# A Macaron block on one NeuronCore: two adapter matrices summed by TensorE, bias additions moved, and the last value product split in float32r parts

## The reference, cut to what matters

```python
x = x + 0.5 * ffn(layernorm(x))      # sum over 8 chosen adapters of weights[k] * W[ids[k]], and their biases
x = x + attn(layernorm(x))           # RWKV time mixing with a recurrence over tokens, then channel mixing
x = x + 0.5 * ffn(layernorm(x))      # the same adapters again
# channel mixing: kk = square(relu(xk @ Wck.T)), hidden size 1024
#                 out = sigmoid(xr @ Wcr.T) * (kk @ Wcv.T)
```

## Time and profile before

| | us |
|---|---|
| median of 3 runs | 431.5 (431.36 to 431.73) |
| the profiled execution, its own time | 431.73 |
| its span, first to last instruction | 429.9 |
| PE busy | 417.1 (97%), 2042 instructions |
| DVE / ACT / POOL busy | 367.9 / 329.7 / 185.6 |

### The profile page before, as it was taken

One profiled execution on the slowest core, in us unless ns is written; L12 is line 12 of the kernel. 1 busy time (PEld: TensorE's weight loads), 2 busy tenths in 40 slices (PEclk: granted clock), 3 DMA queues, 4 the chain that ended last, 5 costly groups with the idle time before them and its releaser, 6 DMA issues.

```text
span 429.9 us, 6308 instructions
## 1 busy us (share of the span) xinstructions
PE 417.1 (97%) x2042; PEld 337.0 (78%) x2042; DVE 367.9 (86%) x725; ACT 329.7 (77%) x669; POOL 185.6 (43%) x194
## 2 busy tenths in 40 slices
PE   8989989889999999999999999999999999999996
PEld 8865875568868887798769886888779876988985
DVE  2988989998989999998989998999999898886235
ACT  1157977899799969997899979997999489945420
POOL 1446052727272635635372728263553347033011
PEclk9999999999999999999999999999999999999999
DMA  6992010001000110002000200010000000000101
GB/s 200 376 398 81 2 49 0 0 2 52 0 0 2 57 44 0 0 26 74 2 0 25 74 1 2 0 50 1 2 0 25 26 0 2 25 26 0 50 2 50
DMA packets 15972, 18.52 MB, mean 43 GB/s; under 512 B 1083, under 2 KB 13635, under 8 KB 15939
## 3 DMA queue, kind: packets, MB, share of 16 engines
q1 hardware_dynamic: 14538, 17.05, 11.4%
q10 hardware_dynamic: 1400, 1.07, 0.8%
HBM read 13.92 MB, written 4.19 MB: 42 GB/s over the span
## 4 chain that ended last, share of the span: by engine, by line
PE 77%; DVE 1%; issue 0%; ACT 0%; DVEq 0%
PE pair L484 22%; PE pair L362 10%; PE pair L374 10%; PE pair L458 6%; PE pair L459 6%; PE pair L462 6%; PE pair L352 6%; PE pair L343 4%; PE pair L499 3%; PE pair L428 1%; PE pair L432 1%; PE pair L429 1%; PE pair L514 0%; DVE rwkv L1054 0%; DVE work L1048 0%
## 5 line engine op out<-in xcount | busy, mean ns | idle before, releaser
L484 PE MATMUL pair<-wcv_sb,kk 128*128 128x256 f32 x448 | 100.4, 380 | 0.0
L484 PEld LDWEIGHTS pair<-wcv_sb,kk 128*128 128x128 f32 x448 | 83.8, 190 | 11.3 <-ACT kk L741 0.7
L458 PE MATMUL pair<-xck_hi,wck_hi 128*128 128x512 f32 x128 | 54.4, 425 | 0.0
L462 PE MATMUL pair<-xck_lo,wck_hi 128*128 128x512 f32 x128 | 50.7, 396 | 0.0
L459 PE MATMUL pair<-xck_hi,wck_lo 128*128 128x512 f32 x128 | 50.6, 395 | 0.0
L737 ACT ACTIVATE kk<-pair 128x512 f32<-128x512 f32 x64 | 36.3, 589 | 14.2 <-PE pair L462 13.3
L1349 POOL TENSOR_TENSOR x2b<-xs,bias_bc 128x512 f32<-128x512 f32 (+1 forms) x16 | 21.8, 1364 | 56.6 <-DVE xcr_lo L1127 22.9
L1349 POOL TENSOR_TENSOR x<-x,bias_bc 128x512 f32<-128x512 f32 x14 | 18.1, 1296 | 55.7 <-DVE rwkv L1054 36.3
L741 ACT ACTIVATE kk<-kk 128x512 f32<-128x512 f32 x64 | 35.9, 625 | 0.0
L1389 POOL TENSOR_TENSOR xs<-x,xa 128x512 f32<-128x512 f32 x16 | 20.4, 1273 | 31.6 <-DVE xa L1060 31.0
L1309 POOL TENSOR_TENSOR rstd_x<-vare_x,nhalf 128x4 f32<-128x4 f32 (+2 forms) x26 | 27.3, 1050 | 9.1 <-DVE vare_x L909 7.8
(11 more groups left out here) (173 smaller groups left out, 1119.3 us busy)
## 6 DMA issues: line engine op xcount, KB each, us to landing
x<-in_x_dram SPq DMA_DIRECT2D x8, 512.0 KB, 4.0
out_dram<-xs SPq DMA_DIRECT2D x15, 256.0 KB, 2.1
xt<-in_xt_dram SPq DMA_DIRECT2D x4, 512.0 KB, 8.2
work<-in_ffn_w_dram ACTq DMA_DIRECT2D x4, 256.0 KB, 5.1
work<-in_ffn_w_dram SPq DMA_DIRECT2D x4, 256.0 KB, 5.2
kk<-in_wck_dram SPq DMA_DIRECT2D x1, 1024.0 KB, 9.6
xs<-in_xt_dram SPq DMA_DIRECT2D x2, 512.0 KB, 10.8
wcv_sb<-in_wcv_dram SPq DMA_DIRECT2D x1, 1024.0 KB, 12.5
```

Source lines behind the costliest of these rows:

```text
L458: nc.tensor.matmul(key_bank(n), wck_hi[:, h, cols], xck_hi[:, h, :], start=h == 0, stop=False)
L462: last = nc.tensor.matmul(key_bank(n), wck_hi[:, h, cols], xck_lo[:, h, :], start=False, stop=h == CH - 1)
L484: last = nc.tensor.matmul(bank_of("kv", e, i)[:, t % TB * C:(t % TB + 1) * C], kk[:, n, tok:tok + P], wcv_sb[:, n, :], start=n == 0, stop= ...
```

## The change

It has four parts.

1. **Adapters.** POOL's queue loads adapters 6 and 7, SP and ACT three each (their biases stay where they were). DVE makes four gated copies of the centring matrices (scaled by the gates of adapters 0 and 1) in `normed`, and PE multiplies adapters 0 and 1 by them straight into PSUM; DVE sums only adapters 2 to 7. PE's warm-up is 16 matmuls ahead of this and 8 behind it instead of 40. The bias product and ACT's copy of it come behind the centred matrix instead of ahead.
2. **Statistics.** `ON_ACT` becomes 1: the statistics of batch 1 move from DVE to ACT, behind `setup_second`. The three memsets of the recurrence's pads move behind `bias_to_first`.
3. **Bias sums on POOL in the loop.** Both halves of `bias_to_x(f + 1)` now wait for `den_done` only; the half 0 of `bias_to_x2` moves to the end of the loop's pass, behind `xcr_done`.
4. **Last values.** For batch 7 the product is split: ACT squares each `kk` tile twice (once into `kk_hi`, once in place), DVE subtracts to get `kk_lo`, and the same is done for `Wcv`: ACT copies two `wcv_hi` tiles in the pass before, DVE subtracts in the last pass. `last_values` does three float32r matmuls where it did one float32 matmul. In the last pass ACT's `channel_gate` comes behind all squares.

```diff
-    ON_ACT = 2
+    ON_ACT = 1
+    ON_PE = 2
...
-            load_adapters(sp, range(0, K, 2))
+            load_adapters(sp, (0, 2, 4), (6,))
...
-                warm(3, 40)
+                warm(3, 16)
+                pe.wait_ge(s_gated_centre, 1)
+                for k in range(ON_PE):
+                    pe.wait_ge(s_sel[k], 16)
+                    for a in range(CH):
+                        for h in range(CH):
+                            nc.tensor.matmul(pair[1][:, a, 0:C], gated_centre[k][a != h], sel[:, k, h, :], start=k == 0 and h == 0, stop=False)
+                warm(3, 8)
+                pe.wait_ge(s_ffn_acc, K - ON_PE)
...
+                last.then_inc(s_ffn_ps, 1)
                 pe.wait_ge(s_gate_rows, 1)
                 pe.wait_ge(s_bias_sel, 16 * K)
                 nc.tensor.matmul(pair[0][:, 0, 0:C], gate_rows[:, :], bias_sel[:, :], start=True, stop=True).then_inc(s_bias_ps, 1)
...
+                    high = wcv_hi[n // (HB // 2)][:, n % (HB // 2), :]
                     if t == 0:
-                        pe.wait_ge(sq_done, HB * LAST + n + 1)
-                    last = nc.tensor.matmul(by_tiles(last_bank(LAST_KV, j), j)[:, t - LAST_PARTS[j][0], :], kk[:, n, t * P:(t + 1) * P], wcv_sb[:, n, :],
-                                            start=n == 0, stop=n == HB - 1)
+                        pe.wait_ge(kk_hi_done, n + 1)
+                    nc.tensor.matmul(dst, kk_hi[:, n, tok], high, start=n == 0, stop=False)
+                    nc.tensor.matmul(dst, kk_hi[:, n, tok], wcv_lo[:, n, :], start=False, stop=False)
+                    if t == 0:
+                        pe.wait_ge(kk_lo_done, n + 1)
+                    last = nc.tensor.matmul(dst, kk_lo[:, n, tok], high, start=False, stop=n == HB - 1)
...
-            load_adapters(act, range(1, K, 2))
+            load_adapters(act, (1, 3, 5), (7,))
...
             def setup_first():
+                act.wait_ge(s_ffn_ps, 1)
+                nc.scalar.activation(ffn_t[:, :, :], pair[1][:, :, 0:C], ACT.Copy).then_inc(s_ffn, 1)
                 act.wait_ge(s_bias_ps, 1)
                 nc.scalar.activation(bias_bc[:, :], pair[0][:, 0, 0:C], ACT.Copy).then_inc(s_bias, 1)
...
             setup_second()
+            stats_x(1)
...
+            def last_key_parts(n):
+                act.wait_ge(relu_done, HB * LAST + n + 1)
+                nc.scalar.activation(kk_hi[:, n, :], kk[:, n, :], ACT.Square).then_inc(kk_hi_done, 1)
+                key_square(LAST, n)
...
-                for k in range(K):
+                dve.wait_ge(s_const, 4)
+                for k in range(ON_PE):
+                    for i, centre in enumerate((centre_own, centre_other)):
+                        last = nc.vector.tensor_scalar(gated_centre[k][i], centre[:, :], gates_bc[:, k:k + 1], None, ALU.mult)
+                last.then_inc(s_gated_centre, 1)
+                for k in range(ON_PE, K):
...
             bias_to_first()
-            stats_x(1)
+            pads()
...
+                    last_weight_rest()
+                    for n in range(HB // 2):
+                        last_key_rest(n)
                 if has(e - 1):
                     add_second(e - 1, 0)
...
                 if e == LAST:
+                    for n in range(HB // 2, HB):
+                        last_key_rest(n)
                     break
...
             pool.wait_ge(s_const, 6)
+            load_adapters(pool, (6, 7), biases=False)
...
-                    pool.wait_ge(aa_done, 2 * f + 2)
+                    pool.wait_ge(den_done, 2 * f + 2)
                     bias_to_x(f + 1, 0)
-                    pool.wait_ge(rwkv_done, 2 * f + 2)
                     bias_to_x(f + 1, 1)
...
+                if has(f):
+                    pool.wait_ge(xcr_done, 2 * f + 2)
+                    bias_to_x2(e, 0)
```

More of the change, by code:

```diff
@@ L95, in build @@
         normed = sb("normed", [P, NT, C])
+        gated_centre = [[normed[:, 2 * k + i, 0:P] for i in range(2)] for k in range(ON_PE)]
         thc = sb("thc", [P, NT, C])
@@ L254, in by_tiles, with load_adapters, number @@
             return bank.rearrange("p (t c) -> p t c", t=len(LAST_PARTS[j]))
-        def load_adapters(queue, numbers):
+        def load_adapters(queue, numbers, biases_alone=(), biases=True):
             queue.wait_ge(s_ids, 16)
             held = {}
+            def number(k):
+                held[k] = queue.value_load(ids_row[0:1, k:k + 1], min_val=0, max_val=N_ADAPTERS - 1)
             for k in numbers:
-                held[k] = queue.value_load(ids_row[0:1, k:k + 1], min_val=0, max_val=N_ADAPTERS - 1)
+                number(k)
                 queue.dma_start(sel[:, k, :, :], ffn_w[held[k], :, :].rearrange("(h p) o -> p h o", p=P)).then_inc(s_sel[k], 16)
-            for k in numbers:
+            if not biases:
+                return
+            for k in biases_alone:
+                number(k)
+            for k in (*numbers, *biases_alone):
                 queue.dma_start(bias_sel[k:k + 1, :], ffn_b[held[k], :].rearrange("(a c) -> a c", a=1)).then_inc(s_bias_sel, 16)
@@ L378, in ffn_setup @@
                 pe.wait_ge(s_const, 4)
-                warm(3, 40)
+                warm(3, 16)
[7 more added lines that the diff above has]
+                pe.wait_ge(s_ffn_acc, K - ON_PE)
+                for a in range(CH):
+                    for h in range(CH):
+                        last = nc.tensor.matmul(pair[1][:, a, 0:C], (centre_own if a == h else centre_other)[:, :], ffn_sum[:, h, :],
+                                                start=False, stop=h == CH - 1)
+                last.then_inc(s_ffn_ps, 1)
                 pe.wait_ge(s_gate_rows, 1)
@@ L741, in key_square, with last_weight_high @@
                 nc.scalar.activation(kk[:, n, :], kk[:, n, :], ACT.Square).then_inc(sq_done, 1)
+            def last_key_parts(n):
+                act.wait_ge(relu_done, HB * LAST + n + 1)
+                nc.scalar.activation(kk_hi[:, n, :], kk[:, n, :], ACT.Square).then_inc(kk_hi_done, 1)
+                key_square(LAST, n)
+            def last_weight_high():
+                act.wait_ge(s_wcv, 1)
+                act.wait_ge(xs_done, BANKS * LAST)
+                for i in range(2):
+                    last = nc.scalar.activation(wcv_hi[i][:, :, :], wcv_sb[:, i * HB // 2:(i + 1) * HB // 2, :], ACT.Copy)
+                last.then_inc(s_wcv, 1)
             def channel_gate(e):
@@ L888, in _ @@
                     past_cr(f)
+            key_relu(LAST, 4)
+            for n in range(HB - 5):
+                last_key_parts(n)
+                key_relu(LAST, n + 5)
+            for n in range(HB - 5, HB):
+                last_key_parts(n)
+            channel_gate(LAST)
             for j in range(len(LAST_PARTS)):
```

66 lines of the change are left out of this document (41 added, 25 removed).

## The result

The changed kernel takes **441.39 us** (median of 4 executions, 438.73 to 443.09) against 431.5: 2.21% more, ratio 1.0221 with a 95% interval from 1.0186 to 1.0256. So it is clearly slower, but whether by more than 2% is open. The forecast was 432.2, the range 430.7 to 434.2: too low by 9.2, and outside. The profiled execution is the slowest of the four, 443.09, with a span of 441.4, so what follows accounts for more than the median's 9.9.

The account below looks back on a forecast made before the run. PE's work bounds the kernel (97% busy), so only the start and the last pass can change. Last values -2.25, adapters +0.7 and statistics +2.2 gave +0.65 on the profiled 431.73, so a median of 432.2; range 430.7 to 434.2.

Parts of the forecast that it names:

- The loop's bias sums: In the loop's passes: POOL's earlier additions meet DVE's scans, PE bounds the pass, so nothing; bounds -0.3 and +0.3.
- TensorE's lower clock: Rival in the start: PE's 3.7 us of idle time takes the clock down, costing 1.6 us, 433.8; chance 0.27.
- The adapters' term: In the start: a third queue delays adapters 2 and 3; T, DVE's sum end, 14.9: +0.7, bounds -0.3 and +1.3.
- The last values: In the last pass: 96 float32r instructions replace 64 float32 ones, gain 2.25 us, bounds 1.5 and 2.6.
- starving: Rival in the last pass: ACT and DVE feed the last values 1.3 us late, 433.5; chance 0.08.
- The bias product and its copy leave the way of nothing: In the start: moving both (0.38 us) behind the centring gains nothing, and their later place is covered by a wait.
- The statistics: In the start: POOL awaits ACT's statistics, DVE's norm_first(0) starts at T + 12.5, loss 2.2, bounds 1.9 and 3.0.
- The idle time of PE that follows: Behind first_product(1) in the start: PE stands idle some 3.7 us instead of 1.3.
- The lower level at the start: In the warm-up: matmuls 0.21 us apart, read as PE's 1.2 GHz level, held 4.6 us from 2.1 to 6.7.

Follow-up runs that it names:

- e1: The kernel before with only the last values split (and their low parts on ACT and DVE): 429.89 us, ratio 0.9958.
- e18: The kernel of e1 (only the last values split), run again in a later job: 429.75 us, ratio 0.9940 to the kernel before.
- e2: The kernel before with only the loop's bias sums on POOL moved: 435.75 us, ratio 1.0100.
- e3: The kernel before with only the adapters' part (two by PE, third queue, bias product behind): 435.87 us, ratio 1.0087.
- e7: e3 with the adapters loaded by the two old queues: 432.64 us, ratio 1.0044 to the kernel before.
- e14: e12 with the two old queues and ON_ACT = 2 (DVE keeps batch 1's statistics): 431.08 us, ratio 0.9993 to the kernel before.
- e4: The kernel before with only the statistics of batch 1 moved to ACT (ON_ACT = 1): 436.31 us, ratio 1.0103.
- e12: The whole change with x's two bias additions waiting as in the kernel before: 435.28 us, ratio 1.0059 to the kernel before.
- e6: e4 with 16 unused matmuls on PE ahead of the turn of batch 0: 434.58 us, ratio 1.0075 to the kernel before.
- e15: e14 with 8 unused matmuls in PE's idle time ahead of the turn: 430.06 us, ratio 0.9966 to the kernel before.
- e5: e2 with x's bias additions waiting for the end of DVE's scans: 436.37 us, ratio 1.0115 to the kernel before.
- e9: The kernel before with only the first half of x2's bias addition moved, x's waits restored: 431.82 us, ratio 0.9997.
- e10: The kernel before plus one GpSimd addition of two SBUF tensors per pass, beside DVE's scans: 434.85 us, ratio 1.0065.
- e11: As e10, but the extra GpSimd operation is a multiply-add by constants reading one tensor: 432.29 us, ratio 1.0005 to the kernel before.

## Why the prediction was wrong

Two steps failed. The loop's bias sums were costed at nothing and measured +4.1 alone. And TensorE's lower clock was left out of the sum, as a rival with one fall; it fell three times. The adapters' term was too small as well.

**The last values: right.** Forecast -2.25 (bounds -1.5 and -2.6); -1.8 in e1, -2.3 in e18, -1.8 in the tail of the whole change, and no starving.

**The loop's bias sums: wrong, the largest miss of a term.** The step read: "earlier biases meet DVE's scans instead of its additions ... PE bounds the pass, so nothing; bounds -0.3 and +0.3". It measured +4.1 (e2; two of its five executions, 436.95 and 437.3, have clocks of 0.995 and 0.996, and the profiled one, with 0.999, took 435.01, +3.4). I saw what would meet what, and costed the meeting at nothing, since I treated two engines as independent. It mattered because DVE has only a few tenths of slack in a pass before `rwkv`, although PE's idle time and DVE's 43.29 of 46.40 suggest 3 us: the slack of the share isn't slack in the chain.

**The adapters: mis-sized.** Forecast +0.7 by T at 14.9 (bound +1.3). T was 15.5 in e3 and 16.2 in the whole change: DVE started on adapter 2 at 10.6 to 11.7 and not at 10. The direction was right, and e7 shows that the third queue makes it: with two queues it starts at 8.42. That adapters 6 and 7 compete for the full engines fits, but no run separates it from other effects of the third queue. "The bias product and its copy leave the way of nothing" was wrong as well: behind the centring they cost 1.0 in e3, and in e14 all that DVE's shorter sum gave.

**The statistics: right in mechanism and size, but for the clock.** Forecast T + 12.5, +2.2; the whole change had 30.10 - 16.19 = 13.9, of which 1.7 is the slow centring, and e4 27.54 - 14.45 = 13.1. The idle time of PE that follows was put at 3.7; by the prediction's own terms it is 1.3 + 2.2 = 3.5, and 3.22 was measured.

**The clock: the rival came true, and more often than I priced it.** I gave it 0.27 and 1.6 us for one place. It fell in three: ahead of the centring (idle 3.13, +1.7), ahead of the turn (3.22, +2.5) and at the `rwkv` wait near 104 (1.79). In the profiled executions, by the idle time ahead of it: 1.28 (before), 1.34 (e3) and 1.73 (e12) left it up; 1.79 ahead of the same `rwkv` was followed by a lower clock in the kernel after and not in e2; 2.25 ahead of the same turn was followed by it in e3 and not in e7 and e14; and it was down behind 3.13 and 3.22 (after) and 4.06 (e4). The kernel before isn't free of it: of its 80 executions beside the experiments, 7 took 433.1 to 433.8 with a mean granted clock of 0.993 to 0.996, about as much longer as e14's slower half. The lower level at the start, from which the prediction took its price, is read from the spacing of the matmuls alone: the granted clock of the profile is 1.00 from 0 to 10 us.

The error in the working was to price a late datum by its lateness alone: each such wait is paid twice, once as idle time and again at the lower clock. By the profiled execution, 2.0 + 1.7 + 1.9 + 2.5 = 8.1 in the start, 5.2 more up to 415 us and less 1.8 in the tail are the 11.5 of the span. Of the 5.2, `rwkv` shows 3.4 by 151.45 (139.95 before), with the clock's third fall in it, and the passes behind it 0.54 each; e2 divides the 3.4. Its pass that ends near 141 takes 46.90 and the kernel before's 46.03, with the clock up in both; the kernel after's takes 48.57 (102.88 to 151.45). So about 1.7 of it is the clock, and the rest, 0.9 in this pass and 0.9 in the one before, is the collision. Rows of `rwkv` in the kernel before, in e2 and in the kernel after:

```profile
139.95 1.28 DVE L1054 TENSOR_TENSOR rwkv<-work 128x512 f32<-128x512 f32 x2
...
141.42 1.28 DVE L1054 TENSOR_TENSOR rwkv<-work 128x512 f32<-128x512 f32 x2
...
151.45 1.28 DVE L1123 TENSOR_TENSOR rwkv<-work 128x512 f32<-128x512 f32 x2
```

The other three executions of the kernel after had mean granted clocks of 0.982, 0.986 and 0.992 against this one's 0.982, and the last took 438.73. So the clock wasn't down for as long in each, and the median's 9.9 holds less of it.

## What to carry to other kernels

A wait that seems only to delay an addition on GpSimd may be what keeps it away from DVE's operations with two SBUF tensors; before moving one, list what DVE runs in its new place, operand by operand. Cost a wait of TensorE of some 1.8 us or more (the clock was down behind 1.79 in one of two profiles, behind 2.25 in one of three, and behind each of 3 and more) with its second price, the lower clock behind it, and try filling it with idle matmuls (here -1.4 in e6, and a spread of 2.5 us in e14 cut to 0.8 in e15). And a part that is worth nothing by itself (e7) may hold a gain that a reordering in the same part takes away.

## What of the hardware was not expected

A GpSimd addition of 128x512 float32 takes 1.28 alone and 2.19 beside DVE's scans of two SBUF tensors, of which a pair goes from 2.33 to 3.40; with a DVE operand in PSUM neither changes (line 1029 at 670 ns). The Trainium skill, "SBUF — State Buffer", section "Who interferes with whom", says that a DVE instruction with two SBUF inputs contends with a GpSimd instruction that reads SBUF, and that one with at most one SBUF input, outside the 2-port performance modes, does not. The runs agree, e5 and e9 above all; had I weighed it, the loop's term would have been a rival with a price. The same page of the Trainium skill, section "Summary: rules for kernel authors", also says that the second to issue is blocked until the first has finished. The runs come near that but don't show so much: a full wait would make e10's extra addition about 1.0 + 1.28 = 2.3 (an estimate from the scan's start 0.16 ahead of it), and it took 1.89, though spans on GpSimd are rough; and e2's pair of scans with one whole addition between them would take 1.2 + 1.28 + 1.2 = 3.7 (an estimate too) and took 3.40. With one operand (e11) the two scans lost 0.3 together.

How long TensorE was idle doesn't settle by itself whether its clock falls: behind the same 2.25 ahead of the same turn it was up in e7 and e14 and down in e3, and e14's twelve executions of one program fall in two groups, 1.7 apart.
